# Three early loads of a two-convolution kernel move behind the first whole step

## The reference

```
mask = (mean over outputs of |weight| > threshold)       # one value per input channel and tap
x = x + conv3x3(group_norm(x), weight * mask)
x = x + conv5x5(group_norm(x), kernel) + bias            # circular on an image padded by 2: a plain 5x5 convolution
```

## Time and profile before

| | |
|---|---|
| median of 3 runs | 835.81 us (834.25 to 837.2) |
| the profiled execution's own time, and its span | 834.83 us, 833.0 us |
| busy: PE, DVE, ACT, POOL | 757.8, 605.1, 336.1, 266.7 us |
| instructions in the span | 67770 |
| data moved | 150.59 MB, mean 181 GB/s |

### The profile page before, as it was taken

One profiled execution on the slowest core, in us unless ns is written; L12 is line 12 of the kernel. 1 busy time (PEld: TensorE's weight loads), 2 busy tenths in 40 slices (PEclk: granted clock), 3 DMA queues, 4 the chain that ended last, 5 costly groups with the idle time before them and its releaser, 6 DMA issues.

```text
span 833.0 us, 67770 instructions
## 1 busy us (share of the span) xinstructions
PE 757.8 (91%) x32302; PEld 541.3 (65%) x32302; DVE 605.1 (73%) x949; ACT 336.1 (40%) x289; POOL 266.7 (32%) x165
## 2 busy tenths in 40 slices
PE   0585579999999999999999999999999999998795
PEld 0342247787767677777778667867778777766463
DVE  6598368787878879787878788897978785745241
ACT  0352225444443536354444435363634444443410
POOL 1042022233333333232333333332323333333221
PEclk9998879999999999999999999999999999999998
DMA  8979986899897979898998979798987576753124
GB/s 178 209 154 224 218 183 152 192 219 213 194 218 164 221 190 223 195 222 194 219 209 201 213 171 231 177 223 192 221 195 177 138 177 153 155 132 90 43 50 101
DMA packets 234118, 150.59 MB, mean 181 GB/s; under 512 B 18592, under 2 KB 227552, under 8 KB 229984
## 3 DMA queue, kind: packets, MB, share of 16 engines
q1 hardware_dynamic: 228768, 144.67, 78.9%
q10 hardware_dynamic: 4608, 4.23, 2.1%
q0 software_dynamic: 704, 1.25, 0.7%
HBM read 75.60 MB, written 33.59 MB: 131 GB/s over the span
## 4 chain that ended last, share of the span: by engine, by line
PE 87%; issue 4%; DMA 3%; SPq 2%; ACT 1%; DVE 1%; ACTq 0%; POOLq 0%; DVEq 0%; POOL 0%
PE psum L772 66%; PE psum L790 21%; DMA x_bands<-x_dram 1%; DMA mid_bands<-mid 1%; SPq L259 1%; SPq L251 1%; ACT mid_bands L394 0%; DVE bn_in L559 0%; ACTq L455 0%; ACT conv_out L424 0%; ACT x_hi L387 0%; POOLq L57 0%; ACT x_hi L379 0%; SPq L240 0%; SPq L275 0%
## 5 line engine op out<-in xcount | busy, mean ns | idle before, releaser
L360 POOL TENSOR_TENSOR mid<-mid,conv_out 128x512 f32<-128x512 f32 x122 | 246.7, 2052 | 512.3 <-ACT conv_out L424 512.3
L772 PE MATMUL psum<-x_hi,s_hi 32*64 32x512 f16 x6656 | 200.9, 383 | 16.7 <-ACTq L455 6.6
L772 PE MATMUL psum<-x_hi,s_lo 32*64 32x512 f16 x6656 | 198.6, 378 | 1.6 <-issue 1.6
L772 PE MATMUL psum<-x_lo,s_hi 32*64 32x512 f16 x6656 | 198.3, 380 | 0.9 <-issue 0.5
L772 PEld LDWEIGHTS psum<-x_hi,s_hi 32*64 32x64 f16 x6656 | 126.6, 105 | 79.8 <-issue 12.1
L772 PEld LDWEIGHTS psum<-x_hi,s_lo 32*64 32x64 f16 x6656 | 141.7, 104 | 45.8 <-issue 4.6
L772 PEld LDWEIGHTS psum<-x_lo,s_hi 32*64 32x64 f16 x6656 | 105.7, 104 | 79.6 <-issue 10.6
L650 DVE SCALAR_TENSOR_TENSOR mid<-psum,unscale,x_own 128x1024 f32<-128x1024 f32 x64 | 79.2, 1279 | 97.1 <-PE psum L790 96.6
L424 ACT ACTIVATE conv_out<-psum,bias,unscale 128x512 f32<-128x512 f32 x122 | 85.2, 778 | 83.4 <-PE psum L772 83.4
L379 ACT ACTIVATE x_hi<-x_bands 128x2304 f16<-128x2304 f32 x32 | 67.8, 2119 | 119.8 <-PE psum L790 116.9
L387 ACT ACTIVATE x_hi<-mid_bands 128x2560 f16<-128x2560 f32 x32 | 74.8, 2339 | 69.9 <-PE psum L790 67.9
(11 more groups left out here) (77 smaller groups left out, 335.6 us busy)
## 6 DMA issues: line engine op xcount, KB each, us to landing
x_own<-x_dram SPq DMA_DIRECT2D x128, 256.0 KB, 5.0
mid_bands<-mid SPq DMA_DIRECT2D x372, 80.0 KB, 2.7
out_dram<-mid SPq DMA_DIRECT2D x116, 256.0 KB, 5.0
x_bands<-x_dram SPq DMA_DIRECT2D x96, 288.0 KB, 6.1
x_bands<-x_dram SPq DMA_DIRECT2D x32, 272.0 KB, 6.1
mid_bands<-mid SPq DMA_DIRECT2D x124, 64.0 KB, 2.7
every_mv<-mv_scratch ACTq DMA_DIRECT2D x16, 256.0 KB, 4.1
out_dram<-mid SPq DMA_DIRECT2D x24, 128.0 KB, 2.4
```

The costliest lines, as they stand in the source:

```text
L360: nc.gpsimd.tensor_tensor(m, m, conv_out[:, b, :], ALU.add).then_inc(out_added, 1)
L772: ins = nc.tensor.matmul(psum[2 * C * J:2 * C * (J + 1), bank + i, :].rearrange("p (a w) -> p a w", a=A), w[quad(i), at:at + 2, :].rearran ...
```

## The change

Own tile 4 and bands 8 leave the part written by hand, ahead of the loop, and bands 9 no longer load at the head of turn 3. All three now stand in turn 3 behind `move_mid(3)` and ahead of own tile 5, and SP waits for `a5_whole` (end of PE's `singles5` of the first whole step) before the first of them.

```diff
@@ -294,8 +294,6 @@
             load_bands(6)
             load_bands(7)
             move_mid(2)
-            load_own(4)
-            load_bands(8)
 
             for s in range(LAG, STEPS + 1):
                 if has5(s - 1):
@@ -308,7 +306,7 @@
...
-                if has3(s + XB_SLOTS):
+                if s > LAG and has3(s + XB_SLOTS):
                     sp.wait_ge(norm1, s + 2)
                     load_bands(s + XB_SLOTS)
                 if has3(s):
@@ -316,6 +314,11 @@
                         move_edges(s // 2, 1, 0)
                         move_edges(s // 2, 0, 1)
                     move_mid(s)
+                    if s == LAG:
+                        sp.wait_ge(a5_whole, 1)
+                        load_own(LAG + 1)
+                        load_bands(LAG + XB_SLOTS - 1)
+                        load_bands(LAG + XB_SLOTS)
                     if has3(s + X_SLOTS):
                         load_own(s + X_SLOTS)
```

## The result

| | before | changed |
|---|---|---|
| median | 834.72 us (5 runs) | 828.39 us (5 runs) |
| ratio, 95% interval | | 0.9915, 0.990 to 0.993 |
| profiled execution, span | 834.83 us, 833.0 us | 828.39 us, 826.6 us |

A forecast was written before the change was run, and what follows sets the result against it. PE, holding 87% of the chain, was taken to be stopped by code fetches that DMA traffic slows. 834.83 less 7.0 gives 827.8; with the median 1.0 above the profiled run, about 828.8 us, range 825.5 to 834.5.

The forecast's parts named there:

- What bounds the kernel: PE's first whole step: stops of together 17.58 us are PE waiting for 16 KB code blocks, slower when DMA is busy.
- The gain in the first whole step: Code blocks after 91.83 arrive faster with the loads moved; PE's step ends at 112.6 against 119.56, 7.0 us gained.
- The half clock: PE's clock over 100 to 112 in the first whole step: if it still falls once, up to 1.3 us later.
- Both bounds, 1.8 and 9.5: First whole step's gain in us if every code block takes 5.66 us (1.8) or 3.73 us (9.5).
- The stops behind 91.9: Sign in PE's first whole step: stops behind 91.83 shrink from 11.2 us to under 5.
- DVE as a cap: Start of the second step: DVE's chain lets PE begin at 109.9 at best, capping the gain at 9.6 us.
- The wait for `a5_whole`: SP's added wait in turn 3: PE ends `singles5` at about 106, SP arrives about 115, so it costs nothing.
- SP behind PE: After the moved transfers, SP's stores, bands 10 and moves start 5 to 10 us behind PE's pace; costed at nothing.
- rival B: Code comes faster, but surplus traffic meets the exchanges of steps 4 and 6, each taking 2 to 3 us; chance 0.18.
- D: Rival: surplus slows both exchanges like the first, PE stands 7.8 us twice, 8.6 us slower, 844 us; chance 0.08.
- The exchange of the second step: ACT's statistics reading meets the moved loads; slack 3.8 us, a 7.2 us landing costs 3.2; costed nothing, at most 2.
- A: Likeliest case: code comes faster in the first whole step and nothing gives it back; 826.3 to 831.5 us, chance 0.55.

The follow-up runs named there:

- e5: Changed kernel plus 8 unneeded transfers on SP's queue behind the moves of half 2, 2.36 MB of x to spare DRAM in 9 KB pieces; 829.48 us.
- e6: Changed kernel plus 8 unneeded transfers on SP's queue behind the moves of half 2, 2.10 MB to spare DRAM in 512-byte pieces; 828.82 us.
- e3: Changed kernel with the wait for `a5_whole` replaced by one for the normalized half 4, which was long met; 827.48 us.
- the repeat: The changed kernel run again unaltered, on one chip beside two of its variants; 828.08 us.
- e8: Changed kernel with bands 8 and 9 put between the edges and the moves of half 3, own tile 4 left behind the moves; 829.61 us.
- e7: Changed kernel with own tile 4 put between the edges and the moves of half 3, bands 8 and 9 left behind the moves; 826.62 us.

## Why the prediction was right

**What bounds the kernel.** Right. The stops are a wait for blocks of code, made longer by traffic. The prediction read the first half from counts (128 matmuls, 6 blocks of 16 KB) and from the absence of stops in the second pass; the times of the code transfers, each 2.5 to 3.1 us ahead of PE's resumption, bear it out. e5 and e6 show the second half.

**The gain in the first whole step.** 7.0 us was forecast, 8.7 measured. The first interval was 4.86 against an assumed 5.0; the others were 3.48, 3.76 and 3.67 against 4.0, 4.2 and 4.3. I had added for the moves of half 3, but the DMA share is only 0.27 from 100 to 112, and they cost the code little: the two blocks in that time are 0.2 to 0.3 us further apart than the one ahead. The half clock did not come back. Both bounds, 1.8 and 9.5, hold. The stops behind 91.9 shrank to 5.35 us; I had named under 5 as a sign.

**DVE as a cap.** Right: `low3(4)` ran from 110.03 to 112.52 in the changed kernel, as before, and PE used its result at 113.45. 0.9 us of cover were left.

**The wait for `a5_whole`.** Costed at nothing; e3 agrees.

**SP behind PE.** I said 5 to 10 us, it was 9.9. I costed it at nothing because the users of the tiles come late. They did come in time. What I missed in the main case is that SP's lateness shifts the traffic: loads and moves fell onto the exchange of step 6, the fourth whole step. This is rival B, which took 2 to 3 us for each exchange; one exchange cost 1.8 us, and 2.9 in the repeat. The prediction's own sign for B or D, a stop of PE at the head of step 7 for `x_lo`, stands in the row at 183.25.

**The exchange of the second step.** Right that it fits: the reading landed in 4.2 us. I had expected DVE's wait for it to grow; it vanished, since DVE came to it later, at 118.99.

So the sum of 828.8 rests on two terms that were each off by some 1.8 us and cancelled: too small a gain first, and nothing given back later. That it came within 0.4 us of the median is luck; that it came within some 2 us is not. The likeliest case as written, "nothing gives it back", was not what happened; between A and B it was B's mechanism with A's time.

## What to carry to other kernels

When a large piece of code is entered for the first time, look for regular stops that the profile puts to nothing, and at what the DMA engines do in them; loads that aren't needed yet may go behind them. Then ask what the deferred bytes meet: when a burst delays a small transfer with a chain of work behind it, that can take back much of the gain, as 5.2 of 9 us in e8. A gap that is already paced by something else, like SP's own issue of the moves here, may take a part of them: own tile 4 fitted there (e7), bands 8 and 9 did not (e8).

## What the runs showed of the hardware

- Code for PE arrives at one block (128 matmuls with their loads) every 3.5 to 3.8 us in the changed kernel with DMA quiet, and every 3.4 to 4.2 us over all profiles. PE uses up such a block in about 2 us in the 32-column matmuls (a row of 128 in step 5 lasts 2.02 us), so even with DMA quiet the first pass is bound by code there: stops of 1.4 to 1.7 us stayed. The Trainium skill (Runtime: NRT & Kernel Launch, Instruction fetch mechanics) calls the crossing of a block mostly hidden; on the first pass here it is not.
- With DMA full, the transfer of a block started 2.6 to 5.1 us behind PE's resumption, with DMA quiet 1.0 to 1.1 us behind it; it took 1.0 to 1.5 us either way.
- A write of 2 KB in 16-byte pieces took 9.2 us to land behind loads with 9 KB pieces (e8), and 11.4 us in the first whole step of before.
- A stretch mostly of copies from DRAM to DRAM ran at 332 GB/s at a share of 1.04 (e5, 9 KB pieces) and at 290 at 1.02 (e6, 512-byte pieces), where a stretch mostly of loads into SBUF ran at 221 at 1.01.
